# Feed-forward and keys in blocks of one chunk of four batches, and no Gram products of the last chunk

## The reference

```python
x = x + 0.5 * ffn(layernorm(x))
x = x + attn(layernorm(x))
x = x + 0.5 * ffn(layernorm(x))
# ffn: gelu(x @ ternary(W1).T + b1) @ ternary(W2).T + b2, 256 -> 1024 -> 256
# attn, one step per token, A = I and M = 0 at the start, 128x128 per batch:
u = k / (norm(k) + EPS);   Au = A @ u;   denom = 1 + u @ Au
A = A - outer(Au, Au) / denom
M = M + outer(v, sum(k * q) * Au / denom)
o = M @ q
```

## Time and profile before

| | us |
|---|---|
| Median of 3 runs | 1127.75 |
| Lowest and highest run | 1126.37, 1129.62 |
| The profiled execution, its own time | 1127.84 |
| Its span | 1126.1 |
| TensorE busy | 935.5 (83%) |
| VectorE busy | 809.6 (72%) |
| ScalarE busy | 525.0 (47%) |
| GpSimd busy | 300.8 (27%) |

### The profile page before, as it was taken

The page is one execution under the profiler, slowest core; times in us unless marked ns, Lnnn a source line. Parts: engine busy times, 40 slices in busy tenths (PEclk is TensorE's granted clock), DMA queues, the critical chain, the costliest instruction groups (busy, mean ns, idle before and its releaser), DMA issues. The chain is left out here.

```text
span 1126.1 us, 28430 instructions
## 1 busy us (share of the span) xinstructions
PE 935.5 (83%) x11466; PEld 723.1 (64%) x11466; DVE 809.6 (72%) x2568; ACT 525.0 (47%) x1079; POOL 300.8 (27%) x254
## 2 busy tenths in 40 slices
PE   4799999999967688687992355784699999999998
PEld 1467777777754657575891244574567777777766
DVE  6877778787649898786558797977466666666663
ACT  4678878787632042112231032110165656556664
POOL 4345354444210000000000000000575454645440
PEclk9999999999988696789897585776799999999999
DMA  5353554545249351345450000055543342434231
GB/s 151 66 132 104 141 118 136 135 120 150 95 143 227 96 153 51 80 115 150 141 158 1 2 3 4 3 152 123 142 104 94 80 118 67 111 87 104 57 76 56
DMA packets 185518, 113.92 MB, mean 101 GB/s; under 512 B 85808, under 2 KB 178352, under 8 KB 184752
## 3 DMA queue, kind: packets, MB, share of 16 engines
q1 hardware_dynamic: 168496, 95.38, 33.5%
q10 hardware_dynamic: 16896, 16.78, 4.7%
HBM read 49.16 MB, written 37.75 MB: 77 GB/s over the span
## 5 line engine op out<-in xcount | busy, mean ns | idle before, releaser
L1615 POOL TENSOR_TENSOR T<-T,out_bv_rows 128x512 f32<-128x512 f32 x16 | 20.4, 1272 | 471.1 <-DVE out_s_over_d L1718 464.9
L414 DVE TENSOR_TENSOR ffn_h_rest<-ffn_ps_h,ffn_h_high 128x512 f16<-128x512 f32 x128 | 87.2, 686 | 53.6 <-ACT ffn_ps_h L584 53.2
L583 ACT ACTIVATE ffn_h_high<-ffn_ps_h,b_columns 128x512 f16<-128x512 f32 x128 | 87.8, 686 | 65.2 <-PE ffn_ps_h L657 64.7
L1865 PE MATMUL ldl_work<-w_ternary,ldl_panels 128*128 128x256 f16 x512 | 118.2, 273 | 0.0
L671 PE MATMUL ffn_ps_y<-w_ternary,ffn_h_rest 128*128 128x256 f16 x512 | 117.8, 273 | 0.0
L671 PE MATMUL ffn_ps_y<-w_ternary,ffn_h_high 128*128 128x256 f16 x512 | 117.8, 273 | 0.0
L657 PE MATMUL ffn_ps_h<-ffn_xT_high,w_ternary 128*128 128x512 f16 x256 | 98.7, 386 | 11.3 <-DVE ffn_h_rest L414 11.2
L657 PE MATMUL ffn_ps_h<-ffn_xT_rest,w_ternary 128*128 128x512 f16 x256 | 98.6, 385 | 0.0
L1853 PE MATMUL ldl_work<-out_xT_high,w_ternary 128*128 128x512 f16 x256 | 97.0, 379 | 0.0
L1853 PE MATMUL ldl_work<-out_xT_rest,w_ternary 128*128 128x512 f16 x256 | 97.0, 379 | 0.0
L1766 ACT ACTIVATE ldl_work<-ldl_work,b_columns 128x512 f32<-128x512 f32 x128 | 84.1, 657 | 0.0
(11 more groups left out here) (206 smaller groups left out, 2305.8 us busy)
## 6 DMA issues: line engine op xcount, KB each, us to landing
ffn_x<-in_x SPq DMA_DIRECT2D x16, 512.0 KB, 4.9
x_scratch<-ffn_x_out ACTq DMA_DIRECT2D x16, 512.0 KB, 3.3
aT_scratch<-ffn_aT SPq DMA_DIRECT2D x16, 512.0 KB, 5.5
inv_aT<-aT_scratch SPq DMA_DIRECT2D x16, 512.0 KB, 4.7
T<-x_scratch SPq DMA_DIRECT2D x16, 512.0 KB, 3.7
uT_scratch<-ffn_uT SPq DMA_DIRECT2D x16, 256.0 KB, 5.5
inv_uT<-uT_scratch SPq DMA_DIRECT2D x16, 256.0 KB, 4.2
qT_scratch<-inv_qT SPq DMA_DIRECT2D x16, 256.0 KB, 3.0
```

What stands on the lines that cost most here:

```text
L414: nc.vector.tensor_tensor(hl[n % 2][:, f], ps_h[f % 3][:], hh[n % 2][:, f], ALU.subtract).then_inc(hl_done, 1)
L583: nc.scalar.activation(hh[n % 2][:, f], ps_h[f % 3][:], ACT.Gelu, bias=c.b1[:, f:f + 1])
L1615: nc.gpsimd.tensor_tensor(v0[s], v0[s], bv[:].unsqueeze(1).to_broadcast(group), ALU.add).then_inc(biased, 1)
L1865: ins = nc.tensor.matmul(ps_y[t % 2], part[k % 2][:, f, t * P:(t + 1) * P], c.w2[:, f], start=(f == 0 and part is hh), stop=(f == FC - 1 a ...
```

## The change

A block becomes one chunk of four batches: block k holds chunk k // 2 of the batches 0 to 3 (k even) or 4 to 7 (k odd). The four running sums of a block no longer depend on one another. They lie side by side in `KK` and become one addition of 128x512 per block, placed at f = 1. It reads the sums of block k - 2. The last chunk is now blocks 14 and 15; for these neither the Gram products nor the sums are issued (`NSUM` = 14), and the memsets go. Loads of x and stores of x1 fetch and write four pieces of 128 rows from four batches in place of 512 rows on end. The stores of uT, qT and v and the loads of uT address four tiles that lie on end. The norms are now in the order of `KK`, so `s_over_d` needs no reordering.

```diff
-    x_v = src.rearrange("(n t p) d -> n p t d", p=P, t=BT)
-    o_v = dst.rearrange("(n t p) d -> n p t d", p=P, t=BT)
-    uT_v = m.uT.rearrange("(c b) i j -> b i c j", b=BATCH)
+    x_v, o_v = (y.rearrange("(b c t) d -> c t b d", b=BATCH, t=P) for y in (src, dst))
+    uT_v = m.uT.rearrange("(g k) i j -> g i k j", k=HC)
+    NSUM = NBLOCK - BATCH // HC
+
+    def rows(y, n):
+
+        return y[n // 2, :, HC * (n % 2):HC * (n % 2) + HC]
...
-                    sp.dma_start(x[n % 2][:], x_v[n]).then_inc(x_in[n % 2], 16)
+                    sp.dma_start(x[n % 2][:], rows(x_v, n)).then_inc(x_in[n % 2], 16)
...
-                    sp.dma_start(uT_v[k // 2, :, HC * s:HC * s + HC], uT[s][:]).then_inc(uT_stored[s], 16)
+                    sp.dma_start(uT_v[k], uT[s][:]).then_inc(uT_stored[s], 16)
...
-                def prefix(k, j):
-                    if j == 0:
-                        v.wait_ge(p_done, k + 1)
-                        if k == 0:
-                            v.wait_ge(kk_start, 1)
-                    b, chunk = k // 2, HC * (k % 2) + j
-                    if chunk == CHUNKS - 1:
-                        nc.vector.memset(no_sum[:], 0.0).then_inc(kk_done, 1)
-                        return
-                    wait(v, kk_done, HC * k + j)
-                    nc.vector.tensor_tensor(m.KK[:, b + (chunk + 1) * BATCH], ps_p[:, j], m.KK[:, b + chunk * BATCH],
-                                            ALU.add).then_inc(kk_done, 1)
+                def prefix(k):
+                    v.wait_ge(p_done, k + 1)
+                    if k < 2:
+                        v.wait_ge(kk_start, 1)
+                    else:
+                        v.wait_ge(kk_done, k - 1)
+                    nc.vector.tensor_tensor(m.KK[:, HC * k + BATCH:HC * k + BATCH + HC], ps_p[:],
+                                            m.KK[:, HC * k:HC * k + HC], ALU.add).then_inc(kk_done, 1)
...
-                        if f < 3:
-                            for j in ((0,), (1, 2), (3,))[f]:
-                                on(n - 5, prefix, j)
+                        if f == 1 and n - 5 < NSUM:
+                            on(n - 5, prefix)
...
-                    act.dma_start(o_v[n], xo[n % 2][:]).then_inc(stored[n % 2], 16)
+                    act.dma_start(rows(o_v, n), xo[n % 2][:]).then_inc(stored[n % 2], 16)
...
-                    wait(act, p_done, k)
+                    wait(act, p_done, min(k, NSUM))
...
-                    wait(pe, kk_done, HC * k)
+                    wait(pe, kk_done, k)
...
-                        if f == 4:
+                        if f == 4 and n - 4 < NSUM:
                             on(n - 4, gram)
...
-        nc.vector.tensor_tensor(s_over_d[:].rearrange("p (c b) -> p b c", b=BATCH),
-                                s_all[:].rearrange("p (b c) -> p b c", b=BATCH),
-                                m.dinv[:].rearrange("p (c b) -> p b c", b=BATCH),
-                                ALU.mult).then_inc(s_done_all, 1)
+        nc.vector.tensor_tensor(s_over_d[:], s_all[:], m.dinv[:], ALU.mult).then_inc(s_done_all, 1)
```

More of the change, by code:

```diff
@@ L265, in feed_forward_keys @@
         a_bn = sb("a_bn", [P, HC, 6])
-        no_sum = sb("no_sum", [P, 1])
         a_mv = sb("a_mean_var", [P, HC, 2])
@@ L807, in factorise @@
         v_out = [sb(f"v{s}", [P, HC, H]) for s in range(2)]
-        qT_v, uT_v, v_v = (y.rearrange("(c b) i j -> b i c j", b=BATCH) for y in (m.qT, m.uT, m.v))
+        qT_v, uT_v, v_v = (y.rearrange("(g k) i j -> g i k j", k=HC) for y in (m.qT, m.uT, m.v))
         ps_q = psum("ps_q", [P, HC, P])
@@ L919, in load_u @@
             for n in QV_OF[r]:
-                half = slice(HC * (n % 2), HC * (n % 2) + HC)
-                sp.dma_start(uT[:, slot(n)], uT_v[n // 2, :, half]).then_inc(u_in, 16)
+                sp.dma_start(uT[:, slot(n)], uT_v[n]).then_inc(u_in, 16)
         def store_q(n):
-            half = slice(HC * (n % 2), HC * (n % 2) + HC)
             sp.wait_ge(q_done, n + 1)
-            sp.dma_start(qT_v[n // 2, :, half], qT[:, slot(n)]).then_inc(q_stored, 16)
+            sp.dma_start(qT_v[n], qT[:, slot(n)]).then_inc(q_stored, 16)
         def store_v(n):
@@ L930, in store_v @@
             sp.wait_ge(v_done, n + 1)
-            sp.dma_start(v_v[n // 2, :, HC * s:HC * s + HC], v_out[s][:]).then_inc(v_stored[s], 16)
+            sp.dma_start(v_v[n], v_out[s][:]).then_inc(v_stored[s], 16)
         def keep_d(r):
```

## The result

| | before | after |
|---|---|---|
| Median of 4 runs each, us | 1127.88 | 1135.82 |
| Lowest and highest, us | 1126.37, 1129.62 | 1135.39, 1137.31 |
| The profiled execution, its time and its span, us | 1127.84, 1126.1 | 1135.92, 1134.2 |
| VectorE busy, us | 809.6 | 804.4 |

The ratio of after to before is 1.0072 with a 95% interval of 1.0055 to 1.0090: some 8 us slower, where 1128.5 us and "the same" were forecast.

The account below looks back on a forecast made before the run. TensorE's order was taken to bound the full blocks. 1127.84 + 1.0 (clock at the hand-over) - 0.3 (one x load) gave 1128.5 us, own range 1126.5 to 1130.3, 8 in 10 from about 1125.6 to 1131.5.

Parts of the forecast that it names:

- The bound and the period: In the first stage's full blocks TensorE's order sets the pace; the block period stays 18.05 us.
- Prefix sums: In full blocks, 9.5 us of VectorE additions replace 16.5 us; VectorE loses 7.0 us of work, gain 0.
- Gram products of the last chunk: At the first stage's end, leaving out the products of blocks 14 and 15 gains 0, at most 0.2 us.
- the slow ones: Slower rivals: x loads landing late in full blocks (1141 us, chance 0.07) or a late last u store (1131.7 us, 0.05).
- The last u store is at its minimum: At the first stage's end, the last u store already lands in its shortest time, 2.3 us; value 0.
- The rival with the late last store: Last u store lands in 5.5 us, not 2.3; next stage starts 3.2 us later: 1131.7 us, chance 0.05.
- The clock at the hand-over: With fewer products before it, the factorisation's first injection runs at TensorE's low clock, costing 0.9 to 1.1 us, taken as 1.0.
- only term of size: The 1.0 us loss from TensorE's low clock at the first injection, the only sizeable term the prediction found.
- only seldom had it high there: No-clock-loss rival: clock high anyway at the first injection, or seldom high in the old kernel; about 1127.3 us, chance 0.27.
- Addresses: Spaced x loads in the first stage: 0.6 us gained to 1.1 lost, taken as 0.3 gained; other transfers 0.
- a rule against the change: Skill page: widely spaced HBM rows slow copies; x loads of 4.9 us would become 6.2 or 9.8 us.

Follow-up runs that it names:

- e3: The kernel before with only the last chunk's Gram products (32 TensorE instructions) left out; 1132.39 us, ratio 1.0039 to the kernel before.
- e1: The changed kernel with 32 waits already met added to TensorE's program at the end of the first stage; 1129.8 us, ratio 1.0002.
- e5: The changed kernel with 32 waits already met added at the very beginning of TensorE's program; 1127.03 us, ratio 0.9989.
- e9: The kernel of e3 with 32 filler instructions at the beginning of TensorE's program, as in e5; 1127.04 us, ratio 0.9987.
- e2: The changed kernel with the Gram products of blocks 14 and 15 issued again, their results unused; 1127.88 us, ratio 0.9992.
- e12: The kernel before, unchanged, profiled once more; 1129.35 us in one execution.
- e6: The changed kernel with 16 filler instructions at the beginning of TensorE's program; 1131.22 us, ratio 1.0031.
- e7: The changed kernel with TensorE filler: 48 at the start, 24 in the first block, 24 before the last turning, 100 ahead of the second factorisation; 1129.71 us, ratio 1.0017.
- e8: The kernel of e3 with the same filler as e7; 1127.54 us, ratio 1.0001.
- e10: The kernel of e8 with 140 in place of 100 filler instructions ahead of the second factorisation; 1125.04 us, ratio 0.9968.
- e11: The kernel of e7 with 140 in place of 100 filler instructions ahead of the second factorisation; 1124.31 us, ratio 0.9962.
- e4: The changed kernel with 96 filler instructions at the end of the first stage, in place of the 32 of e1; 1136.99 us, ratio 1.0082.

## Why the prediction was wrong

**The bound and the period: right.** The full blocks kept 18.05 us, and VectorE's sums did not bound them.

**Prefix sums: right**, in size (9.5 us for 16.5) and in worth (nothing); only VectorE's busy time fell by 5.2 and not by 7.0 us, since the records overlap.

**Gram products of the last chunk: the step that failed.** "Gain 0, at most 0.2 us" weighed the time of the products and the work around them, and bounded them by nothing but a gain. It left out that taking 32 instructions from an engine's program moves all of its later program against the borders at which it is fetched. That costs 3.7 us at the join of leaves 1 and 2, where the prediction priced nothing. The forecast's search for terms ended at 334 us, because no edit lies behind that. e3 shows the loss with this edit alone, and e1, e5 and e9 show it undone by 32 instructions that do no work. No rival held it; the slow ones were about transfers.

**"The last u store is at its minimum": failed**, by 1.1 us (3.4 for 2.3), and by the same cause, since the piece of program behind the shifted border is now fetched beside the store. The rival with the late last store named the right place and the wrong reason: that the store "has the queues to itself as before" was the sentence against it, and the queue of the instruction fetch is one that it didn't count.

**The clock at the hand-over: a number met by a wrong inference.** The comparison shows the 0.86 us that were put at 1.0, and the injection at the low level in 1.94 us, where 1.96 to 2.00 stood. But the Gram products don't by themselves hold the clock: of the three profiles with all of them in front (before, e2, e12) two run the injection in 1.94 and 1.93 us, at granted clock 0.50. So no run shows the "only term of size" as an effect of the change, and its rival, that the old kernel "only seldom had it high there", was the better reading. (The x8 of the rows behind its ratio are four products of two matmuls each, not eight products; the ratio stays.)

**Addresses: right.** Loads of x land in 3.8, 4.7 and 7.9 us (min, median, max) where they took 4.1, 4.9 and 8.1. The load of block 3 is 0.62 us late and was 0.61. The slower loads that the prediction weighed as a rule against the change did not show.

```profile
DMA to landing us min/median/max: 3.8/4.7/7.9
...
67.42 1.41 DVE L396 BATCH_NORM_STATS2 ffn_bn<-ffn_x 128x6 f32<-128x256 f32 x4 [0.62 <-DMA ffn_x<-in_x]
```

**The sum.** The two profiles differ by 8.1 us: 2.1 up to leaf 0 (1.1 from the store, 0.86 from the clock, 0.1 from a later issue), 3.7 to leaf 2, 0.5 in the two joins beside it, 1.4 to leaf 4, then -1.3 in the second factorisation and 1.7 to the end. The -1.3 can't be put down to position: before, e12, e1 and e5 need 49.4 to 49.8 us to leaf 5 and after 47.85, but e2 and e9, whose programs stand where that of before stands, need 47.92 and 48.20. As a whole the loss is due to position, for e5, which differs from after by 32 instructions that do no work, is at 0.9989. Piece by piece only the join of leaves 1 and 2 and the store are shown, 4.8 us together. The rest of the 8 us I can't place, since the other stretches vary by 1 to 3 us between kernels that stand alike.

**What stays open** is the exact condition on which the next piece is asked for. 31 behind a border is too early (e6) and 47 is enough (before, e1, e2, e5, e9) where TensorE had come to the border without a long stand. Behind a border at which it had stood for 1.9 to 2.3 us, 58 is too early (e7, e8) and 98 enough (e10, e11). The kernel before also waits 6 behind a border for 35.9 us at the first join of the second factorisation, and has no gap at the next border: it crosses that one at 638.20 us and the next packet comes only at 640.41, so that piece was already present. Nor is it a count of executed instructions alone: in before and e5 the packet starts 12 and 14 instructions behind the border, and in e6 TensorE gets 31 behind without one. How far ahead the fetch is seems to depend on what came before, and I didn't find the rule.

## What to carry to other kernels

Count instructions as well as microseconds: an edit that removes or adds instructions of an engine moves all of its later program against the borders at which it is fetched, and where hundreds of 8 ns instructions follow a long wait on the path that sets the end, that can cost or give 4 us a place. When a time moves behind an edit and no stretch near it explains that, look for "issue" gaps at a fixed remainder of the instruction number, and try the edit with as many filler instructions as it took away, at a place where the engine is idle, before judging it. And what one profiled execution shows of the clock at a moment is no base for a term; see it in two.

## What was not expected of the hardware

- TensorE's program comes in packets of 16 KB, 256 instructions; they take 0.9 to 3.0 us each. Where the next one is not ahead, TensorE stands at the border, for 1.5 to 2.3 us at the joins shown here, and goes on 1.2 to 1.4 us after the end of the packet.
- A wait of TensorE does not by itself bring the next piece: in after none was fetched in the 4.2 us of the wait, in e7 none in 8.4 us, while in e11 one was fetched during a wait of 9.2 us.
- With a 16 KB fetch beside it, a store of 256 KB landed 0.8 to 1.8 us later (3.1, 3.4 and 4.1 us in three profiles, 2.3 in the eleven without one).
- A wait that is already met costs TensorE 0.11 us as an instruction (10.6 us for 96 in e4, 14.3 us for 133 recorded ones in e11).
- The granted clock in the same program at the same place differed between two executions. In e12 it fell to 0.50 between 328 and 329 us, while the Gram products ran, and was 0.50 at the injection (331.7 us); in the first profile of the same kernel it fell between 327 and 328 us and was back at 1.00 by 331 us.
